# Deeper slots, a new order of SyncE's reloads and earlier index copies in a graph kernel of gathers, one-hot matmuls and running sums

## What is computed

```python
# layer 0: max over the edges of a target (edge_index[0] = src is the target, dst the source)
h   = relu(concat([x[src], x[dst] - x[src]], 1) @ W + b)
x   = layernorm(x + maximum(segment_max(h, src), 0))
# layer 1: a polynomial of degree 5 in the normalised adjacency
deg  = segment_sum(ones, dst);  norm = deg^-1/2 [src] * deg^-1/2 [dst]
coeffs = softmax(W2 @ relu(W1 @ [mean over nodes, mean, std, N, E] + b1) + b2)
tx = x;  result = coeffs[0] * x
for k in 1..5:  tx = segment_sum(norm * tx[dst], src);  result += coeffs[k] * tx
x   = layernorm(x + result)
```

## Time and profile before

| | us |
|---|---|
| median of three runs (lowest, highest) | 3714.44 (3711.14, 3718.24) |
| the profiled execution's own time | 3714.93 |
| its span, first to last instruction | 3713.2 |
| PE / DVE / ACT / POOL busy | 2021.7 / 2741.5 / 2006.8 / 2396.8 |

### The profile page before, as it was taken

How to read it: one execution, slowest core, us unless ns; L and a number is a source line. 1 busy time by engine, 2 the same in 40 slices (tenths; PEclk the granted TensorE clock), 3 DMA queues, 4 the chain that set the end, 5 groups by cost and what they waited for, 6 DMA issues and landing times. The chain is left out here.

```text
span 3713.2 us, 68756 instructions
## 1 busy us (share of the span) xinstructions
PE 2021.7 (54%) x9855; PEld 1236.3 (33%) x9855; DVE 2741.5 (74%) x12754; ACT 2006.8 (54%) x5043; POOL 2396.8 (65%) x2499
## 2 busy tenths in 40 slices
PE   6997554577777765877677787723333333100000
PEld 5775443344444443544344444311111111000000
DVE  8999999887887875777777777754555566655554
ACT  6998886465665653555555555532555540244443
POOL 5665664455555555777777777736666566577776
PEclk9999999899999995777867777755555555555555
DMA  3312443455555553555555555546676663222221
GB/s 117 103 22 66 109 106 75 115 165 163 163 161 163 167 155 100 145 147 143 141 141 141 141 148 145 144 103 151 165 197 171 182 162 93 77 69 71 72 73 54
DMA packets 691005, 466.71 MB, mean 126 GB/s; under 512 B 364761, under 2 KB 576928, under 8 KB 690845
## 3 DMA queue, kind: packets, MB, share of 16 engines
q1 hardware_dynamic: 582260, 321.43, 31.1%
q0 software_dynamic: 83200, 91.59, 11.3%
q10 hardware_dynamic: 25510, 53.37, 4.6%
HBM read 270.97 MB, written 197.86 MB: 126 GB/s over the span
## 5 line engine op out<-in xcount | busy, mean ns | idle before, releaser
L940 POOL DMA_INDIRECT rec<-rec_sb,pos x392 | 389.0, 992 | 323.7 <-issue 309.0
L1525 POOL DMA_INDIRECT rows_H<-tab,at_H x416 | 396.5, 953 | 217.3 <-issue 162.2
L1092 POOL DMA_INDIRECT nd_M<-nd,at_M x400 | 384.3, 961 | 144.6 <-issue 124.2
L1730 POOL DMA_INDIRECT out_x<-res_L,to_L x392 | 381.1, 972 | 139.4 <-issue 118.5
L1097 POOL DMA_INDIRECT pair_M<-x_ext,at_M x400 | 387.4, 968 | 121.9 <-issue 121.9
L858 PE MATMUL gps<-table,hiT 125*128 125x400 bf16 x1568 | 334.6, 361 | 177.0 <-DVE picked L792 175.9
L1546 ACT ACTIVATE node_H<-node_H,mean,M2n 125x64 f32<-125x64 f32 x800 | 273.6, 426 | 287.8 <-issue 148.6
L1638 PE MATMUL zT_H<-ident,z_H 128*64 128x128 f32 x488 | 148.1, 407 | 450.8 <-issue 343.0
L769 DVE SCALAR_TENSOR_TENSOR eq<-srcbc,recs,mask 128x128 bf16<-128x128 f32 (+3 forms) x392 | 196.0, 553 | 134.3 <-DMA srcbc<-src_rows 134.2
L1119 PE MATMUL back_M<-ident,sums_M 128*128 128x128 f32 x784 | 243.7, 406 | 52.7 <-issue 52.7
L858 PEld LDWEIGHTS gps<-table,hiT 125*128 125x128 bf16 x1568 | 156.6, 105 | 327.7 <-DVE picked L792 209.6
(11 more groups left out here) (295 smaller groups left out, 6618.3 us busy)
## 6 DMA issues: line engine op xcount, KB each, us to landing
tab<-given_M SPq DMA_DIRECT2D x98, 384.0 KB
hibc_f<-dst_hi_rows SPq DMA_DIRECT2D x98, 256.0 KB
hibc<-hi_rows SPq DMA_DIRECT2D x98, 256.0 KB, 3.3
srcbc<-src_rows SPq DMA_DIRECT2D x98, 256.0 KB, 4.4
tab<-given_M SPq DMA_DIRECT2D x98, 256.0 KB
own<-given_M SPq DMA_DIRECT2D x98, 256.0 KB
own_L<-own SPq DMA_DIRECT2D x196, 128.0 KB
x_ext<-wide SPq DMA_DIRECT2D x100, 231.0 KB
```

The lines of the kernel that those rows point to most:

```text
L940: pool.indirect_dma_start(out=d.rec, out_offset=bass.IndirectOffsetOnAxis(ap=pos[:, s, j:j + 1], axis=0), in_=rec[:, s, j, :], in_offset=N ...
L1092: pool.indirect_dma_start(out=nd[:, s, j, :], out_offset=None, in_=d.nd, in_offset=bass.IndirectOffsetOnAxis(ap=at[:, s, j, 0:1], axis=0), ...
L1525: pool.indirect_dma_start(out=rows[:, s, j, :], out_offset=None, in_=gather, in_offset=bass.IndirectOffsetOnAxis(ap=at[:, s, j:j + 1], axi ...
L1730: pool.indirect_dma_start(out=d.out, out_offset=bass.IndirectOffsetOnAxis(ap=to[:, s, j:j + 1], axis=0), in_=res[:, s, j, :], in_offset=No ...
```

## The change

It has four parts.

1. Counting and class stages work in four slots instead of two (`quads`: 24 loops of four groups and a rest of two). The gathers of `x` rows stay in two. `far` now lies in the half of `edge_x` that is filled later; `edge_x` is laid out as two strips. In the class stage TensorE looks two groups ahead instead of one.
2. Each of the three large fills is issued in three pieces.
3. In the placing stage SyncE's load of a chunk moves behind the store of the other slot.
4. In the sum passes the copy of the row numbers is made one slot ahead.

```diff
-TAIL_W = (NPOS + P - ROUNDS * 1024) * 3 * C // P
+TAIL_R = (NPOS + P - ROUNDS * 1024) // P
...
-        edge_x = sb("edge_x", [P, EB, 4, C])
+        edge_x = sb("edge_x", [P, 2, EB, 2, C])
...
-        n_fills = 16 * 5
+        n_fills = 16 * 11
+        def quads(eng, step):
+            with eng.Fori(0, QUADS) as i:
+                for s in range(4):
+                    step(i, s)
+            for s in range(REST):
+                step(QUADS, s)
...
-            ohp = isb("ohp", [P, 2, 4, NROW], BF16)
+            ohp = isb("ohp", [P, 4, 4, NROW], BF16)
...
-            far = isb("far", [P, 2, 4, NROW])
+            far = edge_x[:, 1].rearrange("p a j c -> p (a j c)")[:, 0:16 * NROW].rearrange(...)
...
                 for t, width in ((d.tab[0], 2), (d.tab[1], 3), (d.own, 2)):
-                    act.dma_start(t[ROUNDS * 1024:, :].rearrange("(p r) f -> p (r f)", p=P),
-                                  zeros[:, 0:TAIL_W // 3 * width]).then_inc(fills, 16)
+                    by_row = t[ROUNDS * 1024:, :].rearrange("(p r) f -> p r f", p=P)
+                    for r in range(0, TAIL_R, TAIL_R // 3):
+                        act.dma_start(by_row[:, r:r + TAIL_R // 3, :].rearrange("p r f -> p (r f)"),
+                                      zeros[:, 0:TAIL_R // 3 * width * C]).then_inc(fills, 16)
...
+                def group(i, u):
+                    dst_rows(i, u)
+                    fetch(i * 2 + (u // 2 + 1), u % 2)
+                    act.activation(edge_x[:, 0, ds(i * 4 + u, 1)]..., rows_x[:, u % 2], ACT.Copy
+                                   ).then_inc(kept[u % 2], 1)
...
-            fps = [... for s in range(2)]
+            fps = [... for s in range(4)]
...
                     if ahead:
-                        hot_bytes(i + 1, s)
+                        hot_bytes(i + (s + 2) // 4, (s + 2) % 4)
...
-                look(0, 0)
-                with pe.Fori(0, LAST) as i:
-                    for s in range(2):
-                        look(i + s, 1 - s)
+                for s in range(2):
+                    look(0, s)
+                with pe.Fori(0, QUADS) as i:
+                    for s in range(4):
+                        look(i + (s + 2) // 4, (s + 2) % 4)
                         add(i, s)
...
-                with sp.Fori(0, LAST) as i:
-                    for s in range(2):
-                        rows(i + 1, s)
-                        widened(i, s)
-                        widen(i + 1, s)
-                for s in range(2):
-                    widened(LAST, s)
-                    widen(LAST + 1, s)
-                for s in range(2):
-                    widened(LAST + 1, s)
+                rows(1, 0)
+                widened(0, 0)
+                rows(1, 1)
+                widened(0, 1)
+                widen(1, 0)
+                with sp.Fori(1, LAST) as i:
+                    rows(i + 1, 0)
+                    widened(i, 0)
+                    widen(i, 1)
+                    rows(i + 1, 1)
+                    widened(i, 1)
+                    widen(i + 1, 0)
+                widened(LAST, 0)
+                widen(LAST, 1)
+                widened(LAST, 1)
+                widen(LAST + 1, 0)
+                widened(LAST + 1, 0)
+                widen(LAST + 1, 1)
+                widened(LAST + 1, 1)
...
+            def fetch_next(i, s):
+                fetch(*((i, s + 1) if s + 1 < NS else (i + 1, 0)))
...
+            fetch(0, 0)
             if final:
-                staggered(dve, more, NS, (0, fetch), (2, mix), (4, keep_ahead), (2, weigh_both), (3, running_sum),
+                staggered(dve, more, NS, (0, fetch_next), (2, mix), (4, keep_ahead), (2, weigh_both), (3, running_sum),
                           (2, add_near))
```

More of the change, by code:

```diff
@@ L357, in _, with onehots_of @@
                 dve.memset(zero[:], 0.0).then_inc(zero_ready, 1)
[L358 to L366, removed]
+                def onehots_of(i, u):
+                    dve.wait_ge(oh_used[u], i)
+                    for j in range(4):
+                        t = ds(i * 4 + u + j * EB, 1)
+                        dve.tensor_scalar(ohp[:, u, j], k.iota[:, 0:NROW], hi[:, 0, t], None, ALU.is_equal)
+                        for w in range(2):
+                            last = dve.tensor_scalar(ohc[:, u, j, w], k.iota[:], lo[:, w, t], None, ALU.is_equal)
+                        last.then_inc(oh_ready[u], 1)
+                quads(dve, onehots_of)
                 link = Chain(dve, cch)
@@ L433, in _ @@
                         pe.matmul(cps[w][:, h, 0:NR], zero[:, 0:NP], zero[:, 0:NR], start=True, stop=True)
[L434 to L443, removed]
@@ L444, in _, with add_group @@
-                for u in range(2):
-                    pe.wait_ge(oh_used[u], EB // 2)
+                def add_group(i, u):
+                    pe.wait_ge(dst_ready[u], i + 1)
+                    for j in range(4):
+                        pe.wait_ge(oh_ready[u], i * 4 + (j + 1))
+                        for w, rows in enumerate((ohp, ohd)):
+                            for h in range(2):
+                                last = pe.matmul(cps[2 if w else j // 2][:, h, 0:NR], rows[:, u, j, h::2],
+                                                 ohc[:, u, j, w], start=False, stop=True, skip_group_check=True)
+                    last.then_inc(oh_used[u], 1)
@@ L446, in _ @@
+                quads(pe, add_group)
+                for u in range(4):
+                    pe.wait_ge(oh_used[u], QUADS + (u < REST))
                 pe.sem_inc(counted, 1)
-        hi_in, dist_done, hiT_ready, looked, picked_flag = pairs("hi_in", "dist_done_f", "hiT_ready_f", "looked", "picked_flag")
-        byte_done, shifted, near_ready, flagged, hotq = pairs("byte_done", "shifted", "near_ready", "flagged", "hotq")
-        weighted, added_f, at_ready, gathered, kept = pairs("weighted", "added_f", "at_ready_y", "gathered_y", "kept_y")
+        hi_in, dist_done, hiT_ready, looked, picked_flag = fours("hi_in", "dist_done_f", "hiT_ready_f", "looked", "picked_flag")
@@ L523, in _ @@
                     hot_bytes(0, s)
-                with dve.Fori(0, LAST) as i:
-                    for s in range(2):
+                with dve.Fori(0, QUADS) as i:
+                    for s in range(4):
                         classify(i, s, True)
-                for s in range(2):
-                    classify(LAST, s, False)
+                for s in range(REST):
+                    classify(QUADS, s, False)
                 dve.wait_ge(acted, 1)
@@ L562, in _, with group @@
                     fetch(0, s)
-                with act.Fori(0, EB // 2) as i:
-                    for s in range(2):
[L565 to L568, removed]
+                def group(i, s):
+                    rows(i, s)
+                    fetch(i * 2 + (s // 2 + 1), s % 2)
+                    act.activation(edge_x[:, 1, ds(i * 4 + s, 1)].rearrange("p a j c -> p (a j) c"), rows_x[:, s % 2],
+                                   ACT.Copy).then_inc(kept[s % 2], 1)
+                quads(act, group)
             @block.sync
```

83 lines of the change are left out of this document (40 added, 43 removed).

## The result

The changed kernel took 3633.4 us in the median of four runs (3628.4 to 3638.3), the kernel before 3715.9 us beside it: a ratio of 0.978, 95% interval 0.976 to 0.980. A second set of runs on another chip gave 0.977 (0.976 to 0.979). So it is faster by 82 us, inside the range of the prediction (3555 to 3655), but 47 us short of its number, 3586. The profiled execution has a span of 3628.2 us, 85.0 less than before, and all that follows is read from it.

What follows compares the result with a forecast made beforehand. The prediction took the placing stage to run at the pace of SyncE's order, with a store's landing inside it, 7.27 us a group. Its sum was 3714.9 - 119 + 5 - 15 = 3586 us, range 3555 to 3655.

Steps and rivals of the forecast that it cites:

- The term of 119 us: Placing stage: SyncE's new order takes a group from 7.27 to 6.0 us, 119 us gained over 94 groups.
- I see three loops: Placing stage, what is late next: VectorE 5.72 us a group, the wide load's landing 6.0, the rows 5.7.
- (b): Placing stage: load issued, landing, factor, store, gap to the next load; landing + 1.6 us, taken as 6.0 a group.
- R1: Placing stage: the load's landing takes the store's place, 6.8 us a group, 3661 us (6.5 gives 3633); chance 0.17.
- loop (c): Placing stage: rows issued behind the load, 11.4 us from factor to factor for two groups, 5.7 a group.
- The end of the placing stage, +5: Last two chunks go load, landing, factor, store one after another ahead of nd: 5 us lost (0 to 6).
- The sum passes, -15: Position copies one slot ahead starve POOL less: 14 us gained in four passes, 1 in the last (0 to 22 together).
- Counting and class in four slots, 0: Counting and class stages: ScalarE and VectorE are already full there, so four slots bring 0 us.
- R2: Placing stage: VectorE alone bounds, 5.72 us a group, 3559 us; chance 0.13.
- R3: Placing stage: the load's landing grows as transfers overlap; at 6.0 us landing the kernel is slower, 3736 us; chance 0.03.
- R5: Placing stage does not follow: SyncE's wait only moves from store to factor, only the passes are won, 3705 us; chance 0.02.
- R4: Placing stage: POOL's scatters become the bound beside a busy VectorE, 6.24 us a group, 3608 us; chance 0.05.

Runs made afterwards that it cites:

- rec_and_wide_four: The changed kernel with four slots instead of two for both the record buffers (rec_sb, pos) and the wide tile: 3559.0 us, ratio 0.956 to the kernel before.
- rec_four_slots: The changed kernel with four slots instead of two for rec_sb and pos, a semaphore for each slot: 3563.5 us, ratio 0.957 to the kernel before.
- pos_after_pick: The changed kernel with a group's positions computed right behind its picks in VectorE's order: 3655.5 us, ratio 0.982 to the kernel before.

## Why the prediction was right, and where not

**The bound before.** Right. SyncE's order with a store's landing in it set 7.27 us a group; with the order alone changed, the wait for the store left the trace and 74.5 us with it.

**The term of 119 us.** This is the one that was mis-sized: it measured 93 x (7.27 - 6.50) = 72 us. It failed at the step "I see three loops". There was a fourth, through the two slots of `rec_sb`: landing of the scatters, record copy, `factor`, store, load, rows, ranks, positions, scatters. I had named (b), the load's landing, as last at 6.0. The load never decided: `factor` waited for it 10.9 us in 22 times over the steady part, 0.9 at most, and four slots for the wide tile changed nothing. The agreement of 6.0 with the 6.05 of `factor` put first is by chance, since there the records still stood in the way. R1 had the right size (6.5 a group, 3633 us) and the wrong cause, and the time measured fell on it. That the total fell into the range all the same is partly luck: nothing in the prediction priced this loop. The landing that counted was that of the scatter: over the 61 copies that waited for it in the changed kernel, the copy ran 3.1 to 5.0 us, 4.2 in the median, after the last of the four scatters had started. The rows of before had only its 18.8 us, but the code showed it: `records` waits for `scattered` ahead of `factor`. It could have been costed by walking SyncE's new wait at the store back through ScalarE's own order, rather than from `dist` to `factor` as if nothing stood between them, as loop (c) did with its 3.34 us from the stage's start, where no scatter was yet outstanding.

**The end of the placing stage, +5.** Right: from the last row pair to `nd` were 21.8 us before and 26.4 after, +4.6, with loads, factors and stores one after another, 4.7 us a turn (stores at 1318.18, 1322.94 and 1327.67). `nd` went out at 1328.51, and the last scatter had started at 1323.95. But `rec_and_wide_four` showed the cover under it: the scatters would hold the end of the stage to within a microsecond or so once groups come at VectorE's pace.

**The sum passes, -15.** Right: 14.8 us in the trace (19.3 less 4.5), 16.3 alone on the chip. The split was nearly so: the first four passes gave 15.0 us from their first to their last gathers, where 14 were forecast, and the last pass 5.4, not 1, of which some 2 were left at VectorE's end of it. In the first four passes POOL now runs back to back from first to last gather (H5: 72 gathers in 88.7 us, 1.25 each, where 90.8 were before), as here in H2:

```profile
2712.04 0.94 POOL L1553 DMA_INDIRECT rows_H<-tab,at_H  x1 [10.91 <-DVE at_H L1594]
2713.28 0.94 POOL L1553 DMA_INDIRECT rows_H<-tab,at_H  x1 [0.30 <-issue]
2714.53 0.94 POOL L1553 DMA_INDIRECT rows_H<-tab,at_H  x1 [0.30 <-issue]
```

**Counting and class in four slots, 0.** Right within the runs' resolution: ratio 1.0003 (0.9994 to 1.0013).

**The rivals.** R2 is what the stage does once the ring is open: 5.76 a group against the floor of 5.72 that the stage's start had shown. R3 did not come. R5 had it right that SyncE's wait would move to `factor` (from 52.6 us to 287.7), but the groups still came 0.77 us faster. R4, POOL slowed beside a full VectorE, can be judged where VectorE works 100.00 of 100 us: the scatters of `rec_four_slots` took 973 ns in the median against 972 before, 1720 at most, 1022 in the mean against 991 from 720 to 1220 us, and did not set the pace: POOL worked 70.75 of 100 us. The Trainium skill ("SBUF — State Buffer", section "SBUF: two separate sides") ties the lockout to particular forms of VectorE's operations; a VectorE that is always busy cost the scatters 31 ns in the mean here.

**What the profile was to show.** The wait for the store gone: yes. Row pairs some 6.0 us apart: 6.50, and "over 6.5" was named as the sign of being wrong; it came out on that line. `eq` waiting under 0.3 us a group: 0.66 (65.0 / 98). A new wait at `factor` for the wide load: 19.9 us in all, 9.0 of them in the last two groups. The clock: 0.95 in the placing stretch, where 0.96 was before, and 1.00 with four record slots. It was also 1.00 in `pos_after_pick` at 6.72 us a group, so the pace of a group does not hang on it.

## What to carry to other kernels

When a wait is taken out of a queue, follow the next instruction that can wait through the program order of every engine on its way, and list every rotating buffer with its number of slots: a ring's time is the sum of its steps over the number of groups that it spans, and it hardly shows in a trace as long as a longer one hides it (18.8 us here). An instruction that others wait for does not belong behind a wait that it does not need; here one move of 0.20 us of work was worth 1.3%, and two more slots of a small tile 2%. And an order that looks late (positions after the next ranks) may cover an engine's wait for its own result, here 0.31 us a group.

## What was unexpected of the hardware

A scatter of 128 rows into DRAM had landed only 3.1 to 5.0 us, 4.2 in the median, after POOL had started it, and 3.2 in the median after its instruction had ended (in the piece above 1014.54 + 1.06 = 1015.60, and the copy at 1018.85), while the DMA engines together moved 180 GB/s. The prediction had no landing of a scatter in it at all. The Trainium skill ("DMA: Bandwidth & Descriptors", section "Anatomy of one DMA — SWDGE (gpsimd) path") gives some 2 us of fixed cost for such a DMA; here the whole was twice that, counted from the start. And VectorE, given an operation that needs the result of the one right before, stood 0.31 us for it (22.8 us in 73 times, `pos_after_pick`).
